# Moving the second layer norm of blocks 0 to 6 into the mixer phase, and summing feed-forward groups into three partial tiles

## What is computed

```python
h = _layernorm(x) * (1 + ca) + sa                       # first norm
x = x + ga * _L0_attn_ref(h, w_qkv, w_swiglu, w_out)    # "the mixer"
h = _layernorm(x) * (1 + cb) + sb                       # second norm
x = x + gb * _L0_ffn_ref(h, gate_up_packed, ..., down_packed, ...)

def _L0_attn_ref(x, ...):
    q, k, v = split(_rms(x) @ w_qkv.T);  q, k = _rms(q), _rms(k);  w = exp(k)
    y = sigmoid(q) * (cumsum(w * v) / (cumsum(w) + 1e-6))
    u, g = split(y @ w_swiglu.T)                        # 2 x 2048 wide
    return x + u * silu(g) @ w_out.T

def _L0_ffn_ref(x, ...):                                # fp4 weights, groups of 128 inputs
    gate, up = split(x @ dequant(gate_up).T)            # 2 x 1408 wide, a scale per group
    y = (silu(gate) * up) @ dequant(down).T
    return y / sqrt(mean(y * y) + eps)
```

## Time and profile before

| | us |
|---|---|
| median of the timed runs | 2038.09 (2038.05 to 2041.14) |
| span of the profiled execution, first to last instruction | 2036.9 |
| median less span | 1.2 |
| PE busy in the span | 1888.6 (93%) |
| DVE, ACT, POOL busy | 1382.7, 921.8, 959.1 |
| phase mixer / phase feed-forward | about 0 to 1401.5 / 1401.5 to 2036.9 |

### The profile page before, as it was taken

How to read it: one execution, slowest core, us unless ns; L and a number is a source line. 1 busy time by engine, 2 the same in 40 slices (tenths; PEclk the granted TensorE clock), 3 DMA queues, 4 the chain that set the end, 5 groups by cost and what they waited for, 6 DMA issues and landing times. The chain is left out here.

```text
span 2036.9 us, 25294 instructions
## 1 busy us (share of the span) xinstructions
PE 1888.6 (93%) x8376; PEld 826.3 (41%) x8376; DVE 1382.7 (68%) x1795; ACT 921.8 (45%) x1421; POOL 959.1 (47%) x680
## 2 busy tenths in 40 slices
PE   4638999999999999999999999998999999999996
PEld 1213444444444444444444444443443433433432
DVE  6996884884874866777678457245657768768756
ACT  4445334333423433523432421122776776776773
POOL 0553422421522521431441231213889889989974
PEclk7869999999999999999999999998999999999998
DMA  8223012012012012101101101313101011011011
GB/s 308 83 68 95 24 35 81 11 39 93 5 40 95 6 35 67 40 26 54 62 26 37 60 6 47 112 35 127 63 1 63 22 42 63 22 42 62 0 42 62
DMA packets 62147, 112.06 MB, mean 55 GB/s; under 512 B 4464, under 2 KB 20848, under 8 KB 61424
## 3 DMA queue, kind: packets, MB, share of 16 engines
q1 hardware_dynamic: 62064, 111.06, 16.3%
HBM read 80.11 MB, written 30.93 MB: 55 GB/s over the span
## 5 line engine op out<-in xcount | busy, mean ns | idle before, releaser
L532 PE MATMUL bank<-Y,wsw 128*128 128x512 f16 x3072 | 684.0, 379 | 8.7 <-DVE late L843 8.4
L786 POOL TENSOR_TENSOR late<-late 128x512 f16<-128x512 f32 x128 | 192.1, 1501 | 633.1 <-ACT late L661 633.0
L532 PEld LDWEIGHTS bank<-Y,wsw 128*128 128x128 f16 x3072 | 299.0, 98 | 376.6 <-DVE late L843 12.0
L1621 DVE SCALAR_TENSOR_TENSOR f_A<-bank,gu_s,f_A 128x512 f32<-128x512 f32 x352 | 260.7, 741 | 177.8 <-ACT f_A L1445 166.8
L509 PE MATMUL bank<-late,wout 128*128 128x512 f16 x1536 | 352.4, 379 | 3.6 <-POOL late L786 3.5
L1445 ACT ACTIVATE f_A<-bank,gu_s 128x512 f32<-128x512 f32 x352 | 241.6, 687 | 157.6 <-PE bank L1370 139.1
L487 PE MATMUL bank<-H,wqkv 128*128 128x512 f16 x1152 | 260.1, 387 | 37.0 <-DVE H L868 30.9
L1525 POOL TENSOR_TENSOR f_A<-f_A 128x512 f32<-128x512 f32 x176 | 253.9, 1443 | 72.9 <-DVE f_A L1621 72.4
L1335 PE MATMUL bank<-f_HH,f_down_hi 128*128 128x512 f16 x704 | 267.3, 382 | 20.2 <-POOL f_HH L1535 19.7
L843 DVE TENSOR_TENSOR late<-late,bank 128x512 f32<-128x512 f32 x128 | 87.7, 685 | 227.4 <-PE bank L532 206.8
L653 ACT ACTIVATE late<-bank 128x512 f32<-128x512 f32 x128 | 76.4, 597 | 350.1 <-PE bank L532 265.5
(11 more groups left out here) (151 smaller groups left out, 2143.8 us busy)
## 6 DMA issues: line engine op xcount, KB each, us to landing
room<-packed SPq DMA_DIRECT2D x48, 176.0 KB, 2.4
X<-xT SPq DMA_DIRECT2D x8, 1024.0 KB, 6.0
h_scratch<-X SPq DMA_DIRECT2D x8, 1024.0 KB, 4.2
f_X<-x_scratch SPq DMA_DIRECT2D x8, 1024.0 KB, 5.5
f_N<-x_scratch SPq DMA_DIRECT2D x7, 1024.0 KB, 5.5
outT<-f_X SPq DMA_DIRECT2D x7, 1024.0 KB, 4.2
late<-xT SPq DMA_DIRECT2D x24, 256.0 KB, 2.9
HR<-h_scratch SPq DMA_DIRECT2D x24, 256.0 KB, 3.2
```

The source lines that it names most:

```text
L532: mm = nc.tensor.matmul(out[:], wsw[:, pw, k, col:col + P], Y[:, px, k, :], start=(k == 0 and pw == 0 and px == 0), stop=(k == DT - 1 and ...
L786: nc.gpsimd.tensor_tensor(UG[:, j % 2, 1, :], G, UG[:, j % 2, 0, :], ALU.subtract).then_inc(UG_low, 1)
L1621: nc.vector.scalar_tensor_tensor(a, EV[ev_bank(j, m)][:], gu_s[:, which * I_T + j, g:g + 1], a, ALU.mult, ALU.add).then_inc(by_dve, 1)
```

## The change

In the mixer, a new set of operations with the prefix `n_` does the second norm of block b-1 during `iteration(b)`, for b = 1 to 7. The residual keeps x1 of a block in a tile X2 of its own, loaded whole; its h part is added during the steps (`residual_h` at steps 9, 10, 14, 15), and `residual` is now four operations instead of eight. The normed block is stored as two fp16 halves in DRAM (`h2_scratch`), and the feed-forward phase loads it into H one block ahead. Only block 7 is still normed in the feed-forward phase, during block 6. `n_reduce` is the same 128 x 512 fp32 matmul against ones as before; it stands behind the 5th and 11th of the 12 groups of `qkv`.

In the feed-forward phase ACT takes groups 0, 2 and 4, DVE groups 1, 3, 5, 6 and 7, into three partial tiles: (0,1), (2,3) and (4,5,6,7). POOL has one `half` a step. `hidden` is POOL's at every step but the last of a block. Without a norm only step 4 uses three banks.

```diff
+        BY_ACT = (0, 2, 4)
+        BY_DVE = (1, 3, 5, 6, 7)
+        PART = (0, 0, 1, 1, 2, 2, 2, 2)
...
+            return range(2, 6) if nxt else range(4, 5) if prev else range(0)
...
-        POOL_STEPS = (1, 2, *range(5, I_T))
+        POOL_STEPS = range(1, I_T)
...
 # mixer, ScalarE
+            def n_sqrt(b):
+                act.wait_ge(n_var, b + 1)
+                nc.scalar.activation(RS2[:], N_BANK[:], ACT.Sqrt, bias=eps[:, 0:1]).then_inc(n_root, 1)
...
                     sqrt(QSQ, b + 1)
+                    if not (isinstance(b, int) and b == 0):
+                        n_sqrt(b - 1)
                     sqrt(KSQ, b + 1)
...
+                    if n == 2 * DT - 2 and not (isinstance(b, int) and b == 1):
+                        n_squares(b - 2)
...
 # mixer, VectorE
+            def n_scale(b):
+                dve.wait_ge(n_root, b + 1)
+                nc.vector.reciprocal(RS2[:], RS2[:]).then_inc(n_recip, 1)
+                dve.wait_ge(n_recip, b + 1)
+                dve.wait_ge(n_squared, DT * (b + 1))
+                for c in range(DT):
+                    nc.vector.scalar_tensor_tensor(X2[:, c, :], X2[:, c, :], mod[:, CB][:, c:c + 1], RS2[:],
+                                                   ALU.mult, ALU.mult).then_inc(n_scaled, 1)
...
+                if s2 and norm:
+                    decode_chunk(b, 0)
+                    n_centre(b - 1)
+                    n_scale(b - 1)
                 if s2:
                     inverse(KSQ, b + 1)
...
                 for j in range(FT):
                     hidden(b, j)
+                    if s2 and norm and j in (2, 4):
+                        n_lower(b - 1, j - 2)
+                        n_lower(b - 1, j - 1)
+                    if s2 and j in (9, 10, 14, 15):
+                        residual_h(b, (9, 10, 14, 15).index(j))
...
 # mixer, GpSimd
+                if norm:
+                    n_adds(b - 1)
                 if s2:
                     add_squares(QSQ, b + 1)
+                    if norm:
+                        n_add_squares(b - 1)
...
 # feed-forward, SyncE
+            def load_H(b, s):
+                if not (isinstance(b, int) and b == 1):
+                    counts(sp, b * 2 * DT * T * 2)
+                    sp.wait_ge(group_done, GROUPS * I_T * (b - 1))
...
 # feed-forward, VectorE
                     for m in range(1, GROUPS, 2):
+                        if m - 1 in BY_DVE:
+                            take(b, j, m - 1, steps)
                         beside(b, s, DT * j + m // 2, prev, nxt)
-                        take(b, j, m)
+                        take(b, j, m, steps)
```

More of the change, by code:

```diff
@@ L379, in iteration @@
             def iteration(b, s1):
+                start = isinstance(b, int) and b == 0
+                last = isinstance(b, int) and b == NB - 1
                 load_words(b, 0)
@@ L396, in iteration @@
                 for k in range(2, CHUNKS):
+                    if not last and k == CHUNKS - 2:
+                        load_h(b, 2)
+                        load_h(b, 3)
                     store_values(b, k)
@@ L399, in iteration @@
                         load_words(b, k + 2)
-                    if not s1 and b == NB - 1 and k == GU_CHUNKS - 1:
+                    if last and k == GU_CHUNKS - 1:
                         sp.wait_ge(qkv_done, QKV * NB)
@@ L404, in iteration @@
                         sp.dma_start(v["values"], v["gu_dram"]).then_inc(values_loaded, 16)
[L405 to L410, removed]
+                        for half in n_stored:
+                            sp.wait_ge(half, 8 * DT)
+                        sp.dma_start(H[:], h2_dram[:, 0]).then_inc(H_loaded, 16)
+                if not last:
+                    store_x1(b)
             iteration(0, True)
@@ L447, in bank_read, with n_reduce @@
                     pe.wait_ge(root[FAMILY[kind]], 2 * b)
+                    if kind == MEAN and not (isinstance(b, int) and b <= 2):
+                        pe.wait_ge(n_root, b - 2)
+            def n_reduce(b, squares):
+                if squares:
+                    pe.wait_ge(n_sq_sum, 3 * (b + 1))
+                    pe.wait_ge(n_centred, DT * (b + 1))
+                else:
+                    pe.wait_ge(n_sum, 3 * (b + 1))
+                    pe.wait_ge(root[0], 2 * NB if isinstance(b, int) and b == NB - 2 else 2 * (b + 3))
+                nc.tensor.matmul(N_BANK[:], ones[:], RS2[:], start=True, stop=True).then_inc(n_var if squares else n_mean, 1)
             def reduce_tiles(kind, b):
@@ L1341, in iteration @@
             def iteration(b, s, prev, nxt):
-                if not first(b):
-                    pe.wait_ge(H_high, DT * b)
-                    pe.wait_ge(H_low, DT * b)
+                steps = r_steps(prev, nxt)
+                if isinstance(b, int) and b == NB - 1:
+                    pe.wait_ge(H_high, DT)
+                    pe.wait_ge(H_low, DT)
+                elif not first(b):
+                    pe.wait_ge(H_loaded, 16 * b)
                 for j in range(I_T):
@@ L1453, in silu @@
             def silu(b, j):
[L1454 removed]
+                act.wait_ge(halves, I_T * b + j + 1)
                 nc.scalar.activation(A[:, slot(j), 0, :], A[:, slot(j), 0, :], ACT.Silu).then_inc(gate_silu, 1)
             def beside(b, s, place, prev, nxt):
[L1458 to L1462 removed]
+                due, c = now(place, COPY_Y)
+                if prev and due:
+                    copy_y(b - 1, c)
+                due, c = now(place, SQUARE_N)
+                if nxt and due:
+                    square_n(c)
+                due, c = now(place, SQUARE_Y)
+                if prev and due:
+                    square_y(b - 1, c)
                 due, c = now(place, HIGH_N)
@@ L1538, in beside @@
             def beside(b, place, prev, nxt):
-                for there, n, start, work in ((nxt, b + 1, ADD_X, add_x), (nxt, b + 1, ADD_N, add_n),
-                                              (prev, b - 1, ADD_Y, add_y)):
-                    due, c = now(place, start, 2)
-                    if there and due and c < NSUM:
-                        work(n, c)
+                due, c = now(place, ADD_X, 2)
+                if nxt and due and c < NSUM:
+                    add_x(c)
+                due, c = now(place, ADD_N, 2)
+                if nxt and due and c < NSUM:
+                    add_n(c)
+                due, c = now(place, ADD_Y, 2)
+                if prev and due and c < NSUM:
+                    add_y(b - 1, c)
             def iteration(b, s, prev, nxt):
```

457 lines of the change are left out of this document (262 added, 195 removed).

## The result

The changed kernel takes 2061.68 us (2060.99 to 2062.45, 4 runs) against 2039.18 (2038.05 to 2041.14, 4 runs) for the kernel before: ratio 1.0108, 95% interval 1.0094 to 1.0123. It is slower, the sign that the forecast held likelier, but by 22.5 us instead of 5, and outside the range of 2028 to 2054.

A forecast was written before the change was run, and what follows sets the result against it. TensorE, busy 93% of the span, was taken as the bound. The mixer would lose 31 us through waits and clock and the feed-forward phase gain 26, so 5 us longer: 2043 us, range 2028 to 2054.

The forecast's parts named there:

- the sign that the forecast held likelier: Whole kernel: slower by more than 0.2% (4 us), chance 0.50, against 0.30 for within and 0.20 for faster.
- the lower halves and `residual_h` [...] fall into steps in which VectorE waits for PE: Mixer: eight VectorE operations of 0.7 to 1.0 us find cover; without it up to 8 us an iteration.
- Rival 3: Mixer: ScalarE's squares hold bank copies 1 to 2 us, or an H load is late; 2052; 0.12 together with rival 4.
- The first wait: Mixer, before U1: norm work ahead of `hidden(b, 0)` makes PE wait 5.2 us in each of iterations 1 to 6.
- the wait before U2: Mixer: today's wait, 1.7 us from start to start, goes in iterations 1 to 5.
- The clock term: Mixer: PE's clock drops after each of six long waits, 1.4 us an iteration (bounds 0 and 1.7), 8 in all.
- Rival 1: Mixer: the clock holds through the waits, 22.7 - 26 = -3, giving 2035 us; chance 0.26.
- blocks 1 to 5, sized at 19: Feed-forward: idle time falls from 36 us together to 3.5 a block, gain 19 (bounds 29 and 6).
- The block end: Feed-forward blocks 1 to 5: eleven VectorE operations in a 6.04 us step make the low half late; 2.1 us a block.
- The other blocks: Feed-forward: block 0 gains 7 us, block 6 loses 2 (bounds 0 and 5), block 7 gains 2.
- Rival 2: Feed-forward block ends: freed GpSimd speeds VectorE, 2.0 us more in blocks 1 to 7; gain 40, time 2029; chance 0.20.
- rival 4: Feed-forward: GpSimd's relief reaches no wait, low half bound by VectorE's additions; gain 12, 2057; 0.12 together with Rival 3.

The follow-up runs named there:

- experiment 3: Changed kernel with only the second pair of n_split (ScalarE) and n_lower (VectorE) moved from step 4 to step 5: 2055.20 us, ratio 1.0093.
- experiment 8: As experiment 6, with the first pair of tiles of the norm split in step 3 instead of step 2: 2007.17 us, ratio 0.9849.
- experiment 2: Changed kernel with only the norm's four scalings moved behind hidden(b, 1), its reciprocal left in front: 2055.57 us, ratio 1.0089.
- experiment 4: Changed kernel with reciprocal, scaling and result of block b-1 earlier on VectorE in feed-forward blocks without a norm: 2053.09 us, ratio 1.0081.
- experiment 5: Changed kernel with its mixer kept, but each feed-forward step again in four partial tiles: 2056.20 us, ratio 1.0085.
- experiment 1: Changed kernel with the norm's reciprocal and four scalings moved behind hidden(b, 1) in the mixer: 2044.55 us, ratio 1.0033.
- experiment 6: Changed kernel with the edits of experiment 1, experiment 3 and experiment 4 together: 2019.62 us, ratio 0.9909.

## Why the prediction was wrong

- **The failed step in the mixer: "the lower halves and `residual_h` [...] fall into steps in which VectorE waits for PE", costed at nothing.** An average of 1.7 us of waiting over 112 `hidden` was read as room in each step. In steps 2 and 4, where the lower halves stood, there was not enough; in steps 3 and 5 there was (experiments 3 and 8). The splits on ScalarE that belong to them, ahead of its squares and `high`, had no term at all. Price in the changed kernel: 1.8 us in five iterations, 9 us, from the second pair (experiment 3 took 2.1 an iteration where the clock did the same); the first pair's cost showed only once the early wait was gone. `residual_h`, the other half of the quoted term, showed no cost in any run. The text itself gave 8 us an iteration as the cost without cover but kept no rival for it. Rival 3 had a second wait in the mixer, at the copies inside Q, K, V; that place had no wait at all.
- **The first wait was right.** PE waits 0.64 + 4.56 = 5.20 us from start to start, predicted 5.2. The scalings measured 2.7 on VectorE (and 2.9 at PE by experiment 2), the reciprocal 3.35, the wait before U2 is gone.
- **The clock term was a little small.** 1.4 was taken from bounds of 0 and 1.7; it is 1.7 in iterations 2 to 6, as nothing of the low stretch fell into the gap, and about 2.5 in iteration 1 (swiglu 137.1 instead of 136.3): 2.6 us more. Rival 1 (the clock holds) is refuted. The HAM oscillation rule of the Trainium skill ("TensorE: Matmul & The Clock Gate") is borne out here: the price was paid anew at each of the six long waits. The sum is 31 + 9 + 2.6 = 42.6, against 42.3 in the swiglu stretches.
- **The failed term in the feed-forward phase: blocks 1 to 5, sized at 19, gave 10.1** (381.9 us before, 363.2 after, less 8.6 of column sums). The block end was sized at 2.1 and is 3.3, from start to start: 0.40, 1.48 and 0.40 in the last step and 0.98 at the next block's first low half. Steps 2 and 3 hold 1.2 where 0.7 was put, and block 4 has 1.6 more at the loop's jump. The text counted eleven VectorE operations in the last step and took 2.1 all the same; experiment 4 shows that the result's place there was the cost (2.2 us a block when it is moved), experiment 5 that the fifth addition added 0.5. The lower bound of that term (gain 6) held it.
- **The other blocks:** block 0 gained 10.1 (7 predicted), block 6 lost 2.5 (2), block 7 gained 1.1 (2). Right in sign and near in size.
- **Rival 2** (GpSimd's relief speeds VectorE up at block ends) was wrong: `f_X` went from 1.00 to 1.07 us, although GpSimd was busy 44 instead of 66 us a block. What counted was the moment at which two operations met. 1.75 beside a GpSimd row and 0.68 without one (at 1661.05) stand in the same step, in the kernel before as after; the last `f_X` of a block went from 1.1 to 1.4. The lower halves of step 2 made such a meeting in the mixer (experiment 8). The trace agrees with the Trainium skill ("SBUF — State Buffer", Who interferes with whom) on that.
- **Rivals 3 and 4** come nearest in time (2052 and 2057), but neither happened: rival 3's place had no wait, and rival 4's feed-forward gain of 12 was 18.8.
- **What the range missed.** The mixer was 10 us dearer and the feed-forward gain 7 smaller at the same time; the range took one such case at a time. It was also narrower than its own terms: the lower bound of blocks 1 to 5 alone (gain 6 instead of 19) gives 2056, and rival 4's 2057 lies outside it.

## What to carry over

Before costing a moved operation at nothing, look at its own step on each engine that it is queued on, and at what stands behind it there; a mean wait over all steps is no room. When a wait is taken away, ask what it had been hiding: here 4.2 of 6.3 us came back two to four steps later, and only the edits together (the long chain behind the second product, the pairs of splits in steps 3 and 5, the result off the block's end, the load away from the loop's jump) made the idea worth 37 us. When work is put ahead of an operation, look also at what that one will then run beside. Which engine's share of a sum is the cheap one depends on the order around it: the same four tiles won 5.5 us in one schedule and lost 7.1 in another.

## What was not expected of the hardware

After the jump back of the feed-forward loop VectorE stood still for 6.39 us with only "issue" beside it, while a load of 1 MB was landing; with that load two steps later the stretch without work between the same two rows was 3.56 us and the block 4.3 us shorter. Four products on VectorE took 4.54 us or 6.69 us according to where they stood beside GpSimd's. And the clock fell to 0.50 behind the 2.43 us wait of experiment 1 as it did behind the 4.40 us one of the changed kernel, 3.4 us both times, while behind the 1.5 us wait of experiment 2 and the waits of 0.9 us in experiment 6 it did not fall: the swiglu of experiment 6 has a granted clock of 1.00 throughout.

```profile
837.00:968.20 131.20, 127.83 (x584) 57.14 (x584) 112.09 (x136) 50.77 (x75) 41.72 (x29) 1.00 0.13 42
```
